# Sorting the first mixture's rows by expert, through DRAM, in a decoder layer of one core

## The chip, the core and the metric

The kernel runs on one core of a Trainium2 chip. A core has TensorE (PE, matmuls and transposes into PSUM), VectorE (DVE), ScalarE (ACT), GpSimd (POOL) and SyncE (SP, which here only issues DMAs), each with a queue of its own that runs in order; they wait for each other by semaphores. The time is the device time of one launch in microseconds; the runs given are separate launches.

## The reference, cut to what matters

`x` holds 16 sequences of 128 tokens of 128 features, 2048 tokens in all. Each of the three parts works on a layer norm of `x` and is added to `x`: a state-space layer with a mixture of 4 experts (below), cross-attention, and a second mixture of 8 experts (two for each token, with capacities), of 512 hidden units each.

```python
ssm_out = jnp.swapaxes(ys, 0, 1)              # the scan's output, 128 steps, 16 states
flat = ssm_out.reshape(-1, d)                 # 2048 x 128
routing = jax.nn.softmax(flat @ Wr + br, axis=1)
top1_w = jnp.max(routing, axis=1)
top1_i = jnp.argmax(routing, axis=1)
hid = jax.nn.silu(jnp.einsum('nd,edf->enf', flat, up_w) + up_b[:, None, :])
all_out = jnp.einsum('enf,efd->end', hid, down_w) + down_b[:, None, :]
sel = jnp.take_along_axis(jnp.swapaxes(all_out, 0, 1), top1_i[:, None, None], axis=1)[:, 0, :]
moe_out = (sel * top1_w[:, None]).reshape(Bb, Ll, d)
out = ssm_out + moe_out                       # then a layer norm
```

All four experts are computed for every token there, and one is chosen. Everything is float32.

## The kernel before, in words

The tokens are 16 tiles of 128, in `G` = 4 groups of `GT` = 4 tiles (512 tokens). The scan has 16 states for each group, 64 units in all. One slot k of a hand-written order stands for one unit: VectorE does `scan(k)`, `drive(k + 1)` (input times the broadcast row B) and `read_out(k - 1)` (state times the broadcast row C); TensorE makes the broadcasts (`send_B`, `send_C`, line 1389), two slots ahead for B; GpSimd adds each read-out to `yD` (`add_state`). `read_out(k)` waits until the sum three units back is made (`HC_RING` = 3). Each engine then does in `around(k)` what the tables `pre_at`, `mix_at`, `kv_at` and `att_at` put at this slot: preparation of the next group, the first mixture of the group just scanned, keys and values, attention and routing of the one before. Slots run on to 64 + 22 + 17 without units. Nothing but these tables and the queues sets the order.

The first mixture of group g begins at slot 16(g + 1) + 1, step 0. Its logits are one matmul a tile, `route_first` finds each token's best expert, and `gate_first` makes a gate of 4 columns that is zero but for the chosen expert. TensorE computes all experts for all tokens: 16 up matmuls of 512 columns, one a slot (`up`, line 1398), each followed by a SiLU on ScalarE (`silu`, line 1202), and 16 down tiles of four matmuls (`down`, line 1407), one a slot. `acc` starts as `yD` turned to rows plus gate times bias (lines 1488 and 1490), and VectorE adds gate times output for each expert at steps 9, 13, 17 and 21 (`add_expert`, line 593). The layer norm of `acc`, attention step 0, follows at step 21 in the same slot. All weights are loaded once at the start, into `w1` and `w2`.

For the last two groups the attention's steps are packed by `LATE_STEPS`. Its pieces are `inverse_root` on GpSimd, `normalize` on ScalarE, transposes, scores, exponentials. GpSimd also issues the second mixture's dispatches, indirect DMAs from `xrow` to `slots_in` (line 1060).

## Time and profile before

| | |
|---|---|
| median of 3 runs | 476.17 us (474.03 to 477.69) |
| the profiled execution's own time | 482.02 us |
| its span, first to last instruction | 480.2 us |
| TensorE's mean granted clock | 0.885 of 2.4 GHz |
| busy: PE, DVE, ACT, POOL | 344.7, 292.0, 263.0, 230.6 us |
| DMA traffic | 23.94 MB |

Busy time is summed over the records of an engine without overlap. TensorE's clock is granted at one of two levels, 1.2 or 2.4 GHz (0.5 and 1.0 in the tables); a number between is a stretch with both. A record of a float32 matmul is one of two that the instruction leaves. Times in the rows are microseconds from the span's start.

### The profile page before, as it was taken

How to read it: one execution, taken by the hardware profiler on the slowest of the kernel's cores; microseconds unless marked ns; L12 is line 12 of the kernel's file. 1: busy time of each engine (PE TensorE's matmuls, PEld its weight loads, DVE VectorE, ACT ScalarE, POOL GpSimd, SP SyncE). 2: the span in 40 equal slices, each digit the busy share in tenths (PEclk: the TensorE clock that was granted, in tenths of full speed). 3: DMA queues.
4: the chain of work that ended last, by engine and by line, in shares of the span. 5: the costliest groups of instructions: out<-in, count | busy, mean ns of one | idle time of the engine just before them, and what ended most of it. 6: DMA issues, size and time to landing. Idle time of an engine off the chain costs nothing. (4 is left out here: it accounts for less than half of the span.)

```text
span 480.2 us, 5947 instructions
## 1 busy us (share of the span) xinstructions
PE 344.7 (72%) x1749; PEld 233.6 (49%) x1749; DVE 292.0 (61%) x840; ACT 263.0 (55%) x465; POOL 230.6 (48%) x275
## 2 busy tenths in 40 slices
PE   1427557769896899978999688661537789999460
PEld 0203333346464565645667455561327757767360
DVE  3478988956999799999974245357136012222055
ACT  3554645668887797868537675413224474554021
POOL 4425755543545665464541422716844435455434
PEclk9999965879999899999899988975558899999966
DMA  6999400000000000000000000200120221210243
GB/s 123 290 233 333 124 1 1 0 0 1 1 1 0 2 1 1 1 2 0 1 1 2 0 0 9 81 1 23 50 61 28 77 67 49 76 53 14 78 120 88
DMA packets 29472, 23.94 MB, mean 50 GB/s; under 512 B 5448, under 2 KB 23943, under 8 KB 29440
## 3 DMA queue, kind: packets, MB, share of 16 engines
q1 hardware_dynamic: 27048, 19.50, 14.8%
q0 software_dynamic: 2304, 4.04, 2.5%
q8 instruction: 14, 0.23, 0.2%
q14 instruction: 18, 0.15, 0.1%
q10 hardware_dynamic: 88, 0.03, 0.0%
...
## 5 line engine op out<-in xcount | busy, mean ns | idle before, releaser
L1072 POOL TENSOR_TENSOR yD<-yD,hc 128x512 f32<-128x512 f32 x64 | 84.4, 1318 | 103.5 <-DVE hc L537 97.9
L1398 PE MATMUL bank<-yD,w 128*128 128x512 f32 x128 | 71.9, 645 | 17.1 <-ACT hid L1202 16.2
L502 DVE TENSOR_TENSOR_SCAN h<-a,bank 128x512 f32<-128x512 f32 x64 | 77.8, 1216 | 1.4 <-DVE bank L489 0.5
L1407 PE MATMUL bank<-w,hid 128*128 128x128 f32 x512 | 74.6, 293 | 0.0
L1407 PEld LDWEIGHTS bank<-w,hid 128*128 128x128 f32 x512 | 68.6, 205 | 9.4 <-issue 6.1
L1389 PE MATMUL bank<-rows,selid 99*128 99x512 bf16 x128 | 47.5, 457 | 25.5 <-DVE hc L537 23.4
L1135 POOL DMA_INDIRECT y_rows<-yslot,dest x40 | 39.1, 977 | 37.6 <-DVE yslot L865 22.1
L1202 ACT ACTIVATE hid<-bank,cols 128x512 f32<-128x512 f32 x64 | 43.4, 683 | 18.0 <-PE bank L1398 11.9
L489 DVE TENSOR_TENSOR bank<-bank,u 128x512 f32<-128x512 f32 x64 | 43.8, 684 | 14.5 <-PE bank L1389 14.2
L1060 POOL DMA_INDIRECT slots_in<-xrow,posu x32 | 32.3, 1010 | 32.7 <-DVE locs L684 14.7
L1389 PEld LDWEIGHTS bank<-rows,selid 99*128 99x128 bf16 x128 | 12.8, 106 | 67.4 <-DVE hc L537 47.0
L537 DVE TENSOR_TENSOR hc<-h,bank 128x512 f32<-128x512 f32 x64 | 43.3, 677 | 0.9 <-PE bank L1389 0.9
L1181 ACT ACTIVATE a<-delta,A_sb 128x508 f32<-128x508 f32 x64 | 40.5, 707 | 0.1
L865 DVE TENSOR_TENSOR yslot<-bank,w 128x128 f32<-128x128 f32 x32 | 9.2, 292 | 47.8 <-PE bank L1643 46.6
L593 DVE SCALAR_TENSOR_TENSOR acc<-bank,gate,acc 128x128 f32<-128x128 f32 x64 | 18.0, 344 | 29.5 <-PE bank L1407 29.4
L1338 ACT ACTIVATE hid<-bank,cols 128x512 f32<-128x512 f32 x32 | 22.0, 687 | 24.4 <-PE bank L1643 17.0
L1187 ACT ACTIVATE xrow<-x_tok,nmr,rstd 128x128 f32<-128x128 f32 x48 | 19.7, 482 | 23.2 <-POOL nmr L1037 23.2
L1372 PE MATMUL bank<-ident,xrow 128*128 128x128 f32 x48 | 9.5, 331 | 31.7 <-ACT xrow L1187 31.6
L1398 PEld LDWEIGHTS bank<-yD,w 128*128 128x128 f32 x128 | 20.8, 204 | 20.7 <-ACT hid L1202 18.1
L1643 PE MATMUL bank<-fc,hid 128*128 128x128 f32 x256 | 30.1, 275 | 0.7 <-DVE yslot L865 0.7
L1643 PEld LDWEIGHTS bank<-fc,hid 128*128 128x128 f32 x256 | 29.4, 192 | 1.8 <-issue 1.8
L1631 PE MATMUL bank<-w,fc1T 128*128 128x512 f32 x64 | 29.2, 596 | 1.5 <-ACT w L1320 1.5
...
## 6 DMA issues: line engine op xcount, KB each, us to landing
...
y_rows<-yslot SPq DMA_DIRECT2D x8, 256.0 KB, 5.2
x_tok<-in_x_dram SPq DMA_DIRECT2D x4, 256.0 KB, 3.9
...
yD<-y_rows SPq DMA_DIRECT2D x4, 256.0 KB, 4.4
xT<-y_rows SPq DMA_DIRECT2D x4, 256.0 KB, 5.7
out_dram<-acc SPq DMA_DIRECT2D x4, 256.0 KB, 2.3
```

Source lines behind the costliest of these rows:

```text
L489: do(v.tensor_tensor(drive_of(k), drive_of(k), grp(u, g), ALU.mult))
L502: ins = v.tensor_tensor_scan(state_of(k), decay_of(k).rearrange("p j n -> p (j n)"), drive_of(k), 0.0, ALU.mult, ALU.add)
L537: do(v.tensor_tensor(read_of(k), state_of(k), bank[C_BANK][:, 0:width(k // NS)], ALU.mult))
L1060: pool.indirect_dma_start(slots_in[:], bass.IndirectOffsetOnAxis(ap=posu[:, r, i:i + 1], axis=0), xrow[:, i, :], None, bounds_check=SLOTS - 1,
L1072: pool.tensor_tensor(grp(yD, g), grp(yD, g), read_of(k), ALU.add).then_inc(summed, 1)
L1135: pool.indirect_dma_start(y_rows[:], bass.IndirectOffsetOnAxis(ap=to, axis=0), yslot[:, half, j * P:(j + 1) * P], None, bounds_check=2 * T ...
L1181: act.activation(decay_of(k)[:, :, 1:P], tiles3(grp(delta, g))[:, :, 1:P], ACT.Exp, scale=A_sb[:, s:s + 1]).then_inc(a_done, 1)
L1202: act.activation(hid[:, m % 2, f, 0:width(g)], bank[UP_BANKS[f % 2]][:, 0:width(g)], ACT.Silu, bias=cols[:, C_UPB + i:C_UPB + i + 1]).then ...
L1389: pe.matmul(bank[b][:, 0:width(g)], selid[:, row:row + 1].to_broadcast([3 * NROW, P]), rows[:, p % 2, at_col:at_col + width(g)], start=Tru ...
L1398: pe.matmul(bank[UP_BANKS[f % 2]][:, 0:width(g)], w1[:, e, f * P:(f + 1) * P], grp(yD, g), start=True, stop=True).then_inc(up_ps, 1)
L1407: ins = pe.matmul(bank[DOWN_BANK][:, j * P:(j + 1) * P], hid[:, m % 2, f, j * P:(j + 1) * P], w2[:, e, f, :], start=(f == 0), stop=(f == F ...
L1643: ins = pe.matmul(bank[4 + t % 2][:, 0:P], hid2[:, e % 2, f, j * P:(j + 1) * P], fc2[:, e, f, :], start=(f == 0), stop=(f == FT - 1))
```

## The change

A group's tokens are sorted by expert into 7 tiles of 128 rows (`MT` = 4 + 4 - 1, enough for any split), and each tile meets only its owner's weights. VectorE makes from a one-hot and two counting matmuls each token's place (`sposu`) and each tile's owner; GpSimd scatters the rows, four indirect DMAs to `srt_in` in DRAM; SyncE reads them back as `xs_tok`, TensorE turns them and ScalarE copies them to `xsT`; each tile takes 4 up matmuls of 128 columns, 4 SiLUs, a bias matmul and 4 down matmuls; the results go by `ys` to `srt_out`, from where four gathers bring the tokens' rows to `back`, and one `add_expert` adds them. `w1` and `w2` are rings of four tiles; SyncE reads a tile's owner into a register and fetches its weights (512 KB) by it, 14.7 MB in all instead of 2 MB. Ups stand at steps 10 to 16, downs at 11 to 17, evictions at 15 and 18, gathers at 19, the add at 23, and the attention starts 25 slots after a group's end instead of 22.

```diff
+MT = GT + E1 - 1
+W_RING = 4
...
+            def sort_places(g):
                 sl = gsl(g)
-                inverse_sum(g, 0)
-                link(one_hot(gate[:, sl, :], sl, 0, 0))
-                do(v.tensor_tensor(gate[:, sl, :], gate[:, sl, :],
-                                   rz[:, 0, sl].unsqueeze(2).to_broadcast([P, SIZES[g], 8]), ALU.mult))
-                at["gate", g] = n[0]
-            def add_expert(g, e):
-                v.wait_ge(dn_ps, downs(g, e + 1))
-                v.wait_ge(init_done, g + 1)
-                v.wait_ge(dve_done, at["acc", g, e - 1] if e else at["gate", g])
+                square = [P, E1, E1]
+                v.wait_ge(cnt_ps, g + 1)
+                cum = bank[MIX_BANK][:, 0:GT * E1].rearrange("p (i e) -> p i e", e=E1)
+                tot = bank[MIX_BANK][:, GT * E1:2 * GT * E1].rearrange("p (i e) -> p i e", e=E1)
+                link(v.tensor_reduce(count1[:], tot.rearrange("p i e -> p e i"), AX.X, ALU.add))
+                link(v.tensor_tensor(cmp1[:], count1[:].unsqueeze(2).to_broadcast(square),
+                                     rows128[:].unsqueeze(1).to_broadcast(square), ALU.is_gt))
+                link(v.tensor_reduce(tiles1[:], cmp1[:], AX.X, ALU.add))
+                link(v.tensor_tensor(cmp1[:], below[:], tiles1[:].unsqueeze(1).to_broadcast(square), ALU.mult))
+                link(v.tensor_reduce(first1[:], cmp1[:], AX.X, ALU.add))
+                link(v.tensor_scalar(off1[:, 0, :], first1[:], float(P), -1.0, ALU.mult, ALU.add))
+                for j in range(GT - 1):
+                    link(v.tensor_tensor(off1[:, j + 1, :], off1[:, j, :], tot[:, j, :], ALU.add))
+                link(v.tensor_tensor(loc1[:], off1[:], cum, ALU.add))
+                at["cnt", g] = n[0]
+                link(v.tensor_tensor(loc1[:], loc1[:], oh1[:], ALU.mult))
+                link(v.tensor_reduce(spos[:], loc1[:], AX.X, ALU.add))
+                link(v.tensor_copy(sposu[:, sl], spos[:]))
+                at["spos", g] = n[0]
+            def sort_owners(g):
+                wide = [P, MT, E1]
+                link(v.tensor_tensor(past1[:], first1[:], tiles1[:], ALU.add))
+                link(v.tensor_tensor(whose[:], iota8[:, 0:MT].unsqueeze(2).to_broadcast(wide),
+                                     past1[:].unsqueeze(1).to_broadcast(wide), ALU.is_ge))
+                link(v.tensor_reduce(owner[:], whose[:], AX.X, ALU.add))
+                link(v.tensor_scalar_min(owner[:], owner[:], float(E1 - 1)))
+                link(v.tensor_copy(owner_no[:, g, :], owner[0:1, :]))
+                at["owner", g] = n[0]
+                do(v.tensor_scalar(owner_col[:, g % 2, :], owner[0:8, :], slot_no[0:8, 0:1], None, ALU.is_equal))
+                link(v.tensor_tensor(whose[:], owner[:].unsqueeze(2).to_broadcast(wide),
+                                     iota8[:, 0:E1].unsqueeze(1).to_broadcast(wide), ALU.is_equal))
+                link(v.tensor_tensor(bias_of[:], whose[:].unsqueeze(2).to_broadcast([P, MT, FT, E1]),
+                                     cols[:, C_UPB:C_UPB + E1 * FT].rearrange("p (e f) -> p f e", f=FT)
+                                     .unsqueeze(1).to_broadcast([P, MT, FT, E1]), ALU.mult))
+                link(v.tensor_reduce(up_bias[:, g % 2, :, :], bias_of[:], AX.X, ALU.add))
+                at["up_bias", g] = n[0]
...
+            def add_expert(g):
+                v.wait_ge(gathered, 16 * GT * (g + 1))
                 for j, i in enumerate(tiles_of(g)):
-                    do(v.scalar_tensor_tensor(acc[:, i, :], bank[DOWN_BANK][:, j * P:(j + 1) * P],
-                                              gate[:, i, e:e + 1], acc[:, i, :], ALU.mult, ALU.add))
-                at["acc", g, e] = n[0]
+                    do(v.scalar_tensor_tensor(acc[:, i, :], back[:, j, :], rz[:, 0, i:i + 1], acc[:, i, :],
+                                              ALU.mult, ALU.add))
+                at["acc", g] = n[0]
...
+            def weights(g, j, e):
+                t = g * MT + j
+                r = t % W_RING
+                if t >= W_RING:
+                    sp.wait_ge(dn_ps, t - W_RING + 1)
+                load(w1[:, r, :], up_w[bass.ds(e, 1), :, :].rearrange("e d f -> d (e f)"), ld_wt[r])
+                load(w2[:, r, :, :], down_w[bass.ds(e, 1), :, :].rearrange("e (t p) d -> p (e t) d", p=P), ld_wt[r])
+            for g in range(G):
+                sp.wait_ge(dve_done, at["owner", g])
+                for j in range(MT):
+                    if j == W_RING:
+                        sp.wait_ge(sorted_in, 16 * GT * (g + 1))
+                        if g:
+                            sp.wait_ge(xs_ps, g)
+                        load(xs_tok, srt_in[g][:].rearrange("(j p) d -> p j d", p=P), ld_rows)
+                    weights(g, j, sp.value_load(owner_no[0:1, g, j:j + 1], min_val=0, max_val=E1 - 1))
+                for half, (lo, hi) in enumerate(((0, GT), (GT, MT))):
+                    sp.wait_ge(evicted, 2 * g + half + 1)
+                    load(srt_out[g][lo * P:hi * P, :].rearrange("(j p) d -> p j d", p=P), ys[:, lo:hi, :], st_rows)
...
+            def sort_rows(g):
+                if g == 0:
+                    pool.wait_ge(cleared, 16 * 2 * G)
+                pool.wait_ge(yrow_done, g + 1)
+                pool.wait_ge(dve_done, at["spos", g])
+                for i in tiles_of(g):
+                    pool.indirect_dma_start(srt_in[g][:], bass.IndirectOffsetOnAxis(ap=sposu[:, i:i + 1], axis=0),
+                                            acc[:, i, :], None, bounds_check=SORTED - 1,
+                                            oob_is_err=False).then_inc(sorted_in, 16)
+            def fetch_rows(g):
+                pool.wait_ge(st_rows, 16 * 2 * (g + 1))
+                if g:
+                    pool.wait_ge(dve_done, at["acc", g - 1])
+                for j, i in enumerate(tiles_of(g)):
+                    pool.indirect_dma_start(back[:, j, :], None, srt_out[g][:],
+                                            bass.IndirectOffsetOnAxis(ap=sposu[:, i:i + 1], axis=0),
+                                            bounds_check=SORTED - 1, oob_is_err=False).then_inc(gathered, 16)
...
+            def silu(g, j):
+                t = g * MT + j
+                act.wait_ge(up_ps, t + 1)
+                if j == 0:
+                    act.wait_ge(dve_done, at["up_bias", g])
+                if t >= 2:
+                    act.wait_ge(dn_ps, t - 1)
+                for f in range(FT):
+                    ins = act.activation(hid[:, t % 2, f, 0:P], bank[UP_BANKS[t % 2]][:, f * P:(f + 1) * P], ACT.Silu,
+                                         bias=up_bias[:, g % 2, j, f:f + 1])
+                ins.then_inc(hid_done, 1)
+            def take_out(g, half):
+                lo, hi = (0, GT) if half == 0 else (GT, MT)
+                act.wait_ge(dn_ps, g * MT + hi)
+                if g:
+                    act.wait_ge(st_rows, 16 * 2 * g)
+                act.activation(ys[:, lo:hi, :], tiles3(bank[DOWN_BANK][:, 0:(hi - lo) * P]), ACT.Copy
+                               ).then_inc(evicted, 1)
...
+            def up(g, j):
+                t = g * MT + j
+                b = bank[UP_BANKS[t % 2]]
+                pe.wait_ge(xsT_done, 2 * (g + 1))
+                pe.wait_ge(ld_wt[t % W_RING], 32 * (t // W_RING + 1))
+                if t >= 2:
+                    pe.wait_ge(hid_done, t - 1)
                 for f in range(FT):
-                    ins = pe.matmul(bank[DOWN_BANK][:, j * P:(j + 1) * P], hid[:, m % 2, f, j * P:(j + 1) * P],
-                                    w2[:, e, f, :], start=(f == 0), stop=(f == FT - 1))
+                    ins = pe.matmul(b[:, f * P:(f + 1) * P], w1[:, t % W_RING, f * P:(f + 1) * P],
+                                    xsT[:, j * P:(j + 1) * P], start=True, stop=True)
+                ins.then_inc(up_ps, 1)
+            def down(g, j):
+                t = g * MT + j
+                o = bank[DOWN_BANK][:, j % GT * P:(j % GT + 1) * P]
+                pe.wait_ge(hid_done, t + 1)
+                if j == 0 and g:
+                    pe.wait_ge(evicted, 2 * g)
+                if j == GT:
+                    pe.wait_ge(evicted, 2 * g + 1)
+                pe.matmul(o, owner_col[0:E1, g % 2, j:j + 1].to_broadcast([E1, P]), bias1[0:E1, :],
+                          start=True, stop=False)
+                for f in range(FT):
+                    ins = pe.matmul(o, hid[:, t % 2, f, 0:P], w2[:, t % W_RING, f, :],
+                                    start=False, stop=(f == FT - 1))
                 ins.then_inc(dn_ps, 1)
...
```

The order on VectorE at the first group's slot 21 (step 4). Before, with `bcm` the preparation of another group:

```order
L436 TENSOR_TENSOR bcm<-bank,bbc_b 128x4x32 [waits rows_ps,ld_w,bc_ps]
L440 TENSOR_REDUCE bcm<-bcm 128x4 [waits dve_done]
L577 TENSOR_REDUCE zs<-ex 128x4 [waits dve_done,ex_done0]
L578 RECIPROCAL rz<-zs 128x4 [waits dve_done]
L561 TENSOR_TENSOR gate<-ixf,iota 128x32 [waits dve_done]
L584 TENSOR_TENSOR gate<-gate,rz 128x32 [waits dve_done]
L502 SCALAR_TENSOR_TENSOR h<-a,bank 128x512 [waits dve_done,a_done]
```

And now:

```order
L624 TENSOR_REDUCE count<-bank 128x4 [waits cnt_ps,dve_done]
L625 TENSOR_TENSOR cmp<-count,rows 128x16 [waits dve_done]
L627 TENSOR_REDUCE tiles<-cmp 128x4 [waits dve_done]
L628 TENSOR_TENSOR cmp<-below,tiles 128x16 [waits dve_done]
L629 TENSOR_REDUCE first<-cmp 128x4 [waits dve_done]
L630 TENSOR_SCALAR off<-first 128x4 [waits dve_done]
L632 TENSOR_TENSOR off<-off,bank 128x4 [waits dve_done] x3
L633 TENSOR_TENSOR loc<-off,bank 128x16 [waits dve_done]
L635 TENSOR_TENSOR loc<-loc,oh 128x16 [waits dve_done]
L636 TENSOR_REDUCE spos<-loc 128x4 [waits dve_done]
L637 CAST sposu<-spos 128x4 [waits dve_done]
L644 TENSOR_TENSOR past<-first,tiles 128x4 [waits dve_done]
```

The gate's two instructions gave way to this chain; eight more for the owners and biases follow, and only then the next scan.

TensorE in the last group's mixture, beside the scores of group 2 (L1536, now L1684). Before:

```order
L1407 MATMUL bank<-w,hid 128x128 [waits dve_done,hid_done]
L1407 MATMUL bank<-w,hid 128x128 x3
L1398 MATMUL bank<-yD,w 128x512 [waits hid_done]
L1536 MATMUL bank<-delta,yD 128x128 [waits k_done,dve_done]
L1536 MATMUL bank<-delta,yD 128x128 x3
```

And now:

```order
L1556 MATMUL bank<-bias,owner_col 128x128 [waits hid_done]
L1559 MATMUL bank<-w,hid 128x128 x4
L1544 MATMUL bank<-xsT,w 128x128 [waits hid_done,ld_wt0,xsT_done]
L1544 MATMUL bank<-xsT,w 128x128 x3
L1684 MATMUL bank<-delta,yD 128x128 [waits k_done,dve_done]
L1684 MATMUL bank<-delta,yD 128x128 x3
```

The down tile of four (L1407) got a bias matmul (L1556) ahead of it, and the up matmul of 512 columns (L1398) became four of 128 (L1544) that wait for the tile's weights and for `xsT`.

GpSimd behind the scan's last add, slots 65 to 71, with `inverse_root` as L1029 to L1037, now L1131 to L1139. Before:

```order
L1072 TENSOR_TENSOR yD<-yD,hc 128x512 [waits dve_done,summed] x5
L1029 TENSOR_SCALAR vpe<-mv 128x4 [waits dve_done]
L1030 TENSOR_SCALAR nmr<-mv 128x4
L1033 TENSOR_TENSOR rstd<-vpe,nhalf 128x4 [waits root_done]
L1037 TENSOR_TENSOR nmr<-nmr,rstd 128x4 [waits root_done]
L1112 COPY acc<-xrow 128x512 [waits normed3]
L1020 TENSOR_TENSOR x_tok<-x_tok,affine 128x512 [waits biased4]
```

And now:

```order
L1195 TENSOR_TENSOR yD<-yD,hc 128x512 [waits dve_done,summed] x2
L1183 DMA back<-srt_out,sposu 128x128 [waits dve_done,st_rows]
L1183 DMA back<-srt_out,sposu 128x128 x3
L1173 DMA srt_in<-acc,sposu 896x128 [waits dve_done,yrow_done]
L1173 DMA srt_in<-acc,sposu 896x128 x3
L1131 TENSOR_SCALAR vpe<-mv 128x4 [waits dve_done]
L1132 TENSOR_SCALAR nmr<-mv 128x4
L1135 TENSOR_TENSOR rstd<-vpe,nhalf 128x4 [waits root_done]
L1139 TENSOR_TENSOR nmr<-nmr,rstd 128x4 [waits root_done]
L1239 COPY acc<-xrow 128x512 [waits normed3]
```

The gathers of group 2, which wait for its store (`st_rows`), and the scatters of group 3 now stand ahead of group 1's `inverse_root`.

## Rows read from the trace of the kernel before

**Rows 1.** The page, its head: busy time of each engine

```profile
span 480.2 us, 5947 instructions
...
PE 344.7 (72%) x1749; PEld 233.6 (49%) x1749; DVE 292.0 (61%) x840; ACT 263.0 (55%) x465; POOL 230.6 (48%) x275
```

**Rows 2.** Busy time by stage, with clock, DMA share, GB/s

```profile
31.00:80.00 49.00, 28.36 (x86) 13.68 (x87) 46.11 (x63) 25.25 (x41) 27.62 (x25) 0.82 0.47 141
80.00:250.00 170.00, 146.94 (x736) 92.31 (x735) 149.49 (x324) 123.40 (x189) 87.15 (x89) 0.94 0.00 1
250.00:322.00 72.00, 58.60 (x324) 43.39 (x323) 29.78 (x163) 38.60 (x72) 22.25 (x31) 0.91 0.04 16
```

**Rows 3.** Who VectorE waited for, 80 to 250 us: total, times, longest

```profile
DVE bank L489 <- PE bank L1389: 13.1, 13, 4.9
DVE acc L593 <- PE bank L1407: 3.9, 6, 1.3
```

**Rows 4.** Groups by form, whole span: busy us, mean ns, idle before

```profile
L1407 PE MATMUL bank<-w,hid 128*128 128x128 f32 x512 | 74.6, 293 | 0.0
L1398 PE MATMUL bank<-yD,w 128*128 128x512 f32 x128 | 71.9, 645 | 17.1 <-ACT hid L1202 16.2 <-POOL yD L1072 0.5 <-issue 0.4
...
L1202 ACT ACTIVATE hid<-bank,cols 128x512 f32<-128x512 f32 x64 | 43.4, 683 | 18.0 <-PE bank L1398 11.9 <-PE bank L1407 5.3
```

**Rows 5.** The chain of waits from 353 us: start, us, what

```profile
353.03 2.28 DMA slots_in<-xrow,posu
...
355.33 3.83 DMA xe_early<-slots_in
...
361.28 1.84 PE bank L1602 x8
...
363.14 1.15 ACT hid L1313 x4
...
364.33 1.16 PE bank L1591 x8
365.49 0.91 PE bank L1602 x8
```

**Rows 6.** VectorE in order of time: start, us, what, idle before

```profile
213.31 1.18 DVE L561 TENSOR_TENSOR gate<-ixf,iota 128x32 f32<-128x32 f32 x1
...
251.27 0.69 DVE L537 TENSOR_TENSOR hc<-h,bank 128x512 f32<-128x512 f32 x1 [0.92 <-PE bank L1389]
...
320.47 1.13 DVE L593 SCALAR_TENSOR_TENSOR acc<-bank,gate,acc 128x128 f32<-128x128 f32 x4 [3.48 <-PE bank L1407]
...
322.95 0.78 DVE L653 TENSOR_TENSOR off<-off,bank 128x16 f32<-128x16 f32 x4
```

**Rows 7.** One line, all its instructions: ns min, median, max; first and last start

```profile
L502 DVE TENSOR_TENSOR_SCAN h<-a,bank x64: 1207/1214/1222, 31.2 to 248.0; 128x512 f32<-128x512 f32 x64
...
L1060 POOL DMA_INDIRECT slots_in<-xrow,posu x32: 969/974/1637, 297.0 to 373.8; - x32
```

**Rows 8.** GpSimd in order of time

```profile
213.17 1.27 POOL L1072 TENSOR_TENSOR yD<-yD,hc 128x512 f32<-128x512 f32 x1
...
326.76 1.64 POOL L1060 DMA_INDIRECT slots_in<-xrow,posu  x1 [1.82 <-DVE locs L684]
328.70 0.97 POOL L1060 DMA_INDIRECT slots_in<-xrow,posu  x1 [0.30 <-issue]
```

**Rows 9.** ScalarE in order of time

```profile
253.49 1.28 ACT L1229 ACT_TABLE_LOAD   x1
...
256.31 1.28 ACT L1202 ACT_TABLE_LOAD   x1
...
281.17 1.65 ACT L1187 ACTIVATE xrow<-x_tok,nmr,rstd 128x128 f32<-128x128 f32 x4 [3.27 <-POOL nmr L1037]
```

**Rows 10.** The page's DMA issues: KB each, us to landing

```profile
out_dram<-acc SPq DMA_DIRECT2D x4, 256.0 KB, 2.3
```

**Rows 11.** Busy time and clock in the tail

```profile
284.00:288.00 4.00, 4.00 (x15) 3.04 (x15) 0.49 (x2) 3.76 (x7) 0.15 (x1) 0.55 0.00 0
```

203 lines of the change are left out of this document (117 added, 86 removed).

## The prediction

> **What bounds the kernel now.** Read the page's first lines and then the table by stage [rows 1, 2]. TensorE is busy 72% of 480.2 us, which invites the thought that halving the mixture's matmuls must pay. The stages say otherwise. From 80 to 250 us, where the scan runs beside a group's mixture, VectorE is busy 149.5 of 170 us and TensorE 146.9: two engines are near their limit, and VectorE's list of waits holds what TensorE costs it, 13.1 us for the broadcasts and 3.9 us for the down matmuls [rows 3]. So in this stage less TensorE work can give 17.0 us at most, and more VectorE work takes back microsecond for microsecond. From 250 to 322 us TensorE is busy 58.6 of 72 us and VectorE 29.8: there the last group's mixture is bound by TensorE. After 322 us the kernel is not touched. The end of the last `add_expert` is the landmark: 320.47 + 1.13 = 321.6 us, which is 69.6 us after the last `read_out` ended at 251.27 + 0.69 = 251.96 [rows 6]. The page's chain of waits starts behind that landmark, so I count the time to it and take the 158 us behind it as they are.
>
> **What the change takes from TensorE.** One up matmul of 512 columns is two records of 645 ns in the mean, one down tile of four matmuls eight records of 293 ns; the starts are closer, since 71.9 and 74.6 us are busy for all 64 and all 64 [rows 4]. Per group that is 18.0 + 18.7 = 36.6 us of records. Instead come 7 tiles. The early feed-forward has the same shapes: four ups in 0.91 us, four SiLUs of 128 columns in 1.15, four downs in 1.16, all at full clock, and 1.84 for the ups at the lower clock [rows 5]. With a fifth matmul for the bias a tile is 0.91 + 1.16 x 5/4 = 2.4 us, a group 16.5, and the 11 transposes and two counts add about 1.3. TensorE is thus relieved of about 19 us a group. ScalarE's work is about even: 16 SiLUs of 683 ns [rows 4] against 28 in 7 x 1.15 = 8.1 us, and three or four evictions more.
>
> **The scan stage, 80 to 250 us.** (a) Waits that go. The longest broadcast wait, 4.9 us, stood where the first group's ups and ScalarE's table loads met; the ups now start ten slots later. It goes, and so do the 3.9 us of `add_expert`. Of the other 8.2 us I keep 7/16, since only 7 of 16 slots hold up and down matmuls: 3.6 us. Gain 17.0 - 3.6 = 13.4 us. (b) VectorE's own work. `choose_expert`, `sort_places` and `sort_owners` are 24 instructions for each group, nearly all chained, on 4 to 112 elements. Four chained ones took 0.78 us, 0.20 each [rows 6]; two wider ones I put at 0.27: 4.9 us, and 0.5 for operands in SBUF while GpSimd adds. (The 32-element one-hot took 1.18 us at 213.31, exactly until GpSimd's add of 213.17 to 214.44 ended [rows 6, 8].) Three groups pay 16.2 us. Out go eight of the ten `add_expert` in this stretch at 1.05 each (they overlap the next scan a little), 8.4 us, the gate's two instructions, 2.4 us over three groups with such waits in them, and one `row_max` that moves behind the scan, 0.6: net +4.8 us. (c) New waits. The chain from `sposu` to `xsT` is four scatters at 1.28, 2.3 to landing, a load that landed in 3.8 at a similar size [rows 5, 8], all in TensorE's queue ahead of the next broadcasts: about 12 us, against four slots of 2.3 (undisturbed) to 3.4 us (the mean of 63 steps from 31.2 to 248.0 [rows 7]). The ends are 0 and, if each group waits two slots, 15 us; I take 1.5 us a group, 4.5, near the low end because broadcasts are sent two slots ahead. Sum: -13.4 + 4.8 + 4.5 = **-4.1 us**.
>
> **The last group, walked by queue from t = 0, the last `read_out`.** Group 2's last down ends at 5, ScalarE evicts it at 7.7 behind the attention's exponentials (1.28 for the table; the next load starts 1.5 us behind it, after four [rows 9]), the store lands at 7.7 + 0.5 + 2.3 = 10.5 [rows 10]. GpSimd has waited for it: four gathers to 15.6, and only then, in its order, the four scatters of group 3 to 20.7. These land at 23.0, the load at 27.2, transposes and two copies end at 29.2. But the copies stand in ScalarE's queue behind a normalisation of group 2 (1.65 [rows 9]) that itself waits for GpSimd's root behind those scatters, so 31. Then seven tiles: TensorE needs 7 x 2.4 = 16.8, the attention of group 2 between them four blocks of 0.9, and ScalarE's queue puts in a normalisation, two table loads and the exponentials ahead of SiLUs, some 5 us: last down at 57. The second `take_out` stands in ScalarE's queue behind `normalize(3, 2)`, which waits for GpSimd's root (1.8), which waits for the eight dispatches of the second mixture (8 x 1.28 = 10.2, from about 46.5): out at 60.7. (The root's 1.8 is an estimate: a few small operations of GpSimd in a chain, between one add of 1.27 [rows 8] and two.) Store 2.8, gathers 5.1, landing 2.3, `add_expert` 1.1: 72.0. Before, 69.6: +2.4 us. This was at full clock. A window of the tail shows a clock of 0.55 with TensorE busy throughout [rows 11], and the walk has two waits of TensorE of more than 3 us. At the lower clock a tile takes some 2 us more, for about two tiles: +4. Sum: **+6.4 us** (from 0 to 15, if all seven tiles run at the lower clock).
>
> **The rest** counts at nothing: the 2 MB of weights no longer loaded at the start and the 1.8 MB that clear `srt_in` both lie under the first scans, whose first start at 31.2 us [rows 7] waits for no weights; cover gone would cost nothing either, as VectorE is busy 46.1 of the 49 us from 31 to 80 [rows 2]. The weights of each tile, 0.5 MB, are fetched four tiles ahead, over 7 us, against 3.8 us to landing for the same size [rows 5].
>
> Together -4.1 + 6.4 = +2.3 us on the profiled execution's 482.0: 484.3. The median of the runs stands at 476.17/482.02 = 0.988 of it: **478.4 us**. One per cent (4.8 us) is about what a measurement of this kernel can tell from no change.
>
> **Rivals.** *Faster.* TensorE was what held both stages, and the new waits find cover: (c) is 0 and nothing of the 8.2 us stays, 17.0 - 4.8 = 12.2 us gained; in the tail the clock holds, and `take_out` is not held behind the dispatches, 3 us less than walked, so -0.6. Time: (482.0 - 12.8) x 0.988 = 463.5 us. For it: TensorE at 58.6 of 72 us in the tail. Against: the walk's end hangs on GpSimd's and ScalarE's order, not on matmuls.
> *Much slower: GpSimd's queue.* GpSimd adds every unit's read-out to `yD`, and `read_out` waits for the add three units back. Four indirect DMAs in its queue hold it for 4 x 1.28 = 5.1 us, and with one add 6.4, less than three slots of 2.3 (63 instructions of VectorE in 49 us, three a slot [rows 2]): no wait. But one such instruction took 1.64 us where VectorE was busy with chained work, against 0.97 [rows 7, 8]. If all take 1.64 + 0.30, a batch holds GpSimd for 7.8 + 1.3 = 9.1 us, 2.1 more than three slots; five batches lie in the scan: +10.7. It decides from 1.4 us an instruction on. Time: (484.3 + 10.7) x 0.988 = 489 us, and 497 with the tail's upper end. For it: VectorE is busy nearly without a gap in the scan. Against: of the 32 such instructions the median is 0.974, the first of a batch alone was long. The Trainium skill's page "SBUF — State Buffer", section "SBUF: two separate sides", speaks against this change at this place: a DMA issued from GpSimd's queue cannot have its descriptors written while VectorE runs an instruction in a two-port mode, and the page advises the SP or ScalarE queue instead. By it the scan's broadcasts and scans are harmless and only copies or casts inside SBUF would hold it; the row of 1.64 shows that something does.
> *The work does not shrink:* matmuls of 128 columns cost what those of 512 did. The row of four ups in 0.91 us speaks against it. It would keep the 13.4 us in place: 492 us.
>
> **Chances.** Forecast, the terms nearly cancel, with its own range of 471 to 485: 0.45. Faster: 0.20. GpSimd's queue: 0.25. The work does not shrink: 0.03; something not on this list, mostly slower: 0.07. Of the forecast's 0.45, 0.33 lie within 1%, 0.10 above, 0.02 below. So faster 0.22, same 0.38, slower 0.40. The range runs from the faster rival to between the queue's two ends: 464 to 495.
>
> **What would show it.** Last scan: 4 us earlier than 248.0 [rows 7] if (a) to (c) are right, 12 earlier for the faster rival, later for the queue's; VectorE's waits would then name GpSimd's add. The distance from the last `read_out` to the end of `add_expert`: 76 us. In it GpSimd's gathers should wait for the store, the scatters stand right behind them, and the second `take_out` behind the normalisation. TensorE's busy time should fall by some 70 us or less, as the clock is lower. Wrong would make me: weights landing late (TensorE waiting on a load of `w`), indirect DMAs that take longer to land while weights stream, or a clock low for whole groups.

## The result: slower by a tenth, and the profile after

The changed kernel takes 523.6 us against 476.9 before. Three of its four runs lie from 522.3 to 524.0 us and one, a slow run that is left out of the ratio, at 537.8. The ratio is 1.098, with an interval of 1.091 to 1.105. Its profiled execution took 523.99 us, 42.0 more than the 482.02 of the one before, with a span of 522.1. The landmarks of [rows 6, 7] part these 42 us:

| us | before | after | forecast for after |
|---|---|---|---|
| last scan starts | 248.0 | 275.7 | 4.1 earlier than before |
| last `read_out` ends | 252.0 | 281.7 | |
| from there to the end of the last `add_expert` (the tail) | 69.6 | 86.9 | 76 |
| from there to the end of the span | 158.6 | 153.4 | 158.6 |

So 29.8 us came in the scan and 17.3 in the tail, and 5.2 went behind it, where nothing was changed. A part of these 5.2 us lies with the profiled execution of the kernel before, whose last stretch was long: in the fourteen experiments, those built on the kernel before among them, this last stretch took 151.0 to 156.3 us.

The page's head and the table by stage of the changed kernel are to be laid beside [rows 1, 2]:

```profile
span 522.1 us, 6051 instructions
...
PE 317.9 (61%) x1585; PEld 228.8 (44%) x1585; DVE 294.6 (56%) x882; ACT 240.3 (46%) x511; POOL 262.6 (50%) x307
...
31.00:80.00 49.00, 26.57 (x86) 12.76 (x85) 46.34 (x63) 24.58 (x41) 27.61 (x25) 0.87 0.48 149
80.00:250.00 170.00, 109.25 (x492) 74.43 (x492) 125.67 (x294) 88.68 (x172) 86.29 (x83) 0.68 0.25 70
250.00:322.00 72.00, 45.74 (x244) 35.46 (x245) 41.97 (x147) 30.35 (x78) 36.68 (x46) 0.69 0.31 89
```

From 31 to 80 us nothing moved. From 80 to 250 us TensorE is busy 109 us instead of 147, and VectorE, which should have had more time, only 125.7 instead of 149.5. The mean granted clock fell from 0.94 to 0.68. A mean over sparse records is rough; the broadcasts show the clock better, 0.60 us for the two records of one at full clock and about 1.04 at the lower. Of those that the timeline shows as a pair between scans 18 and 63, 5 of 45 took the long time before and 29 of 45 after.

VectorE's waits from 80 to 283 us, then TensorE's, are to be laid beside [rows 3]:

```profile
DVE bank L519 <- PE bank L1532: 35.4, 9, 8.8
DVE hc L567 <- PE bank L1532: 3.6, 1, 3.6
```

```profile
PE bank L1532 <- DVE hc L567: 40.0, 22, 7.0
PE bank L1556 <- ACT xe_tok L1340: 9.8, 2, 5.0
PE bank L1544 <- ACT xsT L1416: 6.2, 3, 4.1
PE bank L1556 <- ACT hid L1331: 4.4, 2, 2.2
```

The wait for broadcasts was to shrink from 13.1 us; it is 35.4, in 9 waits. TensorE in turn waits for ScalarE: 9.8 us for the eviction (`ys`, which the trace names `xe_tok`, whose memory it shares, as `xs_tok` shares that of `xe_early`), 6.2 us for the turned rows, 4.4 us for SiLUs. The starts of the scans tell where. The seven slots with tiles, scans 28 to 35 and 44 to 51, take 41.3 and 39.0 us; before, the same scans took 23.7 and 25.8. That is +17.6 and +13.3, together 30.8, more than the 27.7 us by which the last scan is late; scans 0 to 28, 35 to 44 and 51 to 63 changed by -6.3, +3.0 and -0.5.

The longest slot of the first stretch, around the first group's fifth tile, by ScalarE, TensorE and VectorE:

```profile
139.71 1.28 ACT L1308 ACT_TABLE_LOAD   x1
141.01 2.54 ACT L1308 ACTIVATE a<-delta,A_sb 128x508 f32<-128x508 f32 x4
143.57 1.28 ACT L1331 ACT_TABLE_LOAD   x1
144.87 1.14 ACT L1331 ACTIVATE hid<-bank,up_bias 128x128 f32<-128x128 f32 x4
145.88 0.61 ACT L1340 ACTIVATE xe_tok<-bank 128x512 f32<-128x512 f32 x1
...
140.29 1.06 PE L1544 MATMUL bank<-xsT,w 128*128 128x128 f32 x8
141.18 0.60 PE L1532 MATMUL bank<-rows,selid 99*128 99x512 bf16 x2
146.64 0.76 PE L1556 MATMUL bank<-bias,owner_col 4*128 4x128 f32 x2 [4.86 <-ACT xe_tok L1340]
147.33 2.08 PE L1559 MATMUL bank<-w,hid 128*128 128x128 f32 x8
149.20 1.91 PE L1544 MATMUL bank<-xsT,w 128*128 128x128 f32 x8
150.91 1.06 PE L1532 MATMUL bank<-rows,selid 99*128 99x512 bf16 x2
...
143.02 1.21 DVE L532 TENSOR_TENSOR_SCAN h<-a,bank 128x512 f32<-128x512 f32 x1
152.00 0.70 DVE L519 TENSOR_TENSOR bank<-bank,u 128x512 f32<-128x512 f32 x1 [7.77 <-PE bank L1532]
```

ScalarE first loads a table and makes four decays, loads the SiLU's table back, does the tile's SiLUs, and only then `take_out` evicts tiles 0 to 3 (145.88). TensorE's fifth down (its bias matmul, L1556) goes to the same bank and waits 4.86 us for that. When it goes on it is at the lower clock: 2.08 us for a down that otherwise takes 1.16. The next ups and the broadcasts stand behind it in TensorE's queue, and VectorE, idle since its scan at 143.02, waits 7.77 us. Of these, some 2.5 us are the clock's by an estimate from the rows: bias, down, ups and broadcast take 0.76 + 2.08 + 1.91 + 1.06 us here, and 0.48 + 1.16 + 1.06 + 0.60 where the clock is full. The second group's wait at the same place is 4.98 us for TensorE and 8.79 for VectorE.

The tail, by GpSimd, ScalarE, TensorE and VectorE, to be laid beside [rows 6, 8, 9]:

```profile
299.18 1.16 POOL L1183 DMA_INDIRECT back<-srt_out,sposu  x1 [16.02 <-DMA srt_out<-xe_tok]
...
304.56 1.02 POOL L1173 DMA_INDIRECT srt_in<-acc,sposu  x1 [0.30 <-issue]
...
309.59 0.23 POOL L1131 TENSOR_SCALAR vpe<-mv 128x4 f32<-128x4 f32 x1
...
360.93 1.18 POOL L1183 DMA_INDIRECT back<-srt_out,sposu  x1 [1.34 <-DMA srt_out<-xe_tok]
...
311.57 1.65 ACT L1314 ACTIVATE xrow<-x_tok,nmr,rstd 128x128 f32<-128x128 f32 x4 [13.83 <-POOL nmr L1139]
...
356.05 1.65 ACT L1314 ACTIVATE xrow<-x_tok,nmr,rstd 128x128 f32<-128x128 f32 x4 [4.45 <-POOL nmr L1139]
357.60 0.47 ACT L1340 ACTIVATE xe_tok<-bank 128x384 f32<-128x384 f32 x1
...
313.36 1.09 PE L1515 MATMUL bank<-ident,xrow 128*128 128x128 f32 x4 [13.50 <-ACT xrow L1314]
...
319.73 3.69 PE L1544 MATMUL bank<-xsT,w 128*128 128x128 f32 x16 [1.13 <-ACT xsT L1416]
...
367.55 1.14 DVE L663 SCALAR_TENSOR_TENSOR acc<-back,rz,acc 128x128 f32<-128x128 f32 x4 [3.60 <-DMA back<-srt_out,sposu]
```

The order of the walk is there: group 2's gathers wait for the store (16.02 us idle), four scatters stand behind them, group 1's root and normalisation (311.57) behind those, the first ups of the last group at 319.73, and the second `take_out` (357.60) right behind a normalisation that waited for GpSimd. Counted from the last `read_out`, at 281.75, the first gather is at 17.4 (the walk had 10.5), the last down ends at 72.7 (57), the eviction at 76.3 (60.7), the add at 86.9 (72.0).

### The profile page after: what moved, and what is told of

It reads as the page before. It is cut to its first block, busy times and chain, and to the rows that moved or that the text cites. A ratio compares the mean times of both kernels' runs of the same rounds, so it can differ in the third digit from the quotient of the medians.

```text
span 522.1 us, 6051 instructions
## 1 busy us (share of the span) xinstructions
PE 317.9 (61%) x1585; PEld 228.8 (44%) x1585; DVE 294.6 (56%) x882; ACT 240.3 (46%) x511; POOL 262.6 (50%) x307
## 3 DMA queue, kind: packets, MB, share of 16 engines
q1 hardware_dynamic: 55880, 37.59, 25.7%
## 4 chain that ended last, share of the span: by engine, by line
PE 33%; DVE 20%; issue 15%; ACT 14%; POOL 10%; DMA 6%; DVEq 1%; SPq 0%; POOLq 0%; ACTq 0%
PE bank L1791 5%; PE bank L1779 5%; PE bank L1559 4%; PE bank L1544 4%; ACT a L1308 3%; DVE h L532 3%; DVE bank L519 2%; POOL rstd L1135 2%; PE bank L1532 2%; DVE hc L567 2%; ACT hid L1331 2%; ACT L1331 2%; PE bank L1556 1%; ACT xrow L1314 1%; POOL srt_in L1173 1%
## 5 line engine op out<-in xcount | busy, mean ns | idle before, releaser
L1532 PE MATMUL bank<-rows,selid 99*128 99x512 bf16 x128 | 57.9, 548 | 58.9 <-DVE hc L567 56.6
L519 DVE TENSOR_TENSOR bank<-bank,u 128x512 f32<-128x512 f32 x64 | 44.0, 687 | 36.4 <-PE bank L1532 36.1
L1532 PEld LDWEIGHTS bank<-rows,selid 99*128 99x128 bf16 x128 | 13.1, 113 | 81.7 <-DVE hc L567 77.6
L1544 PE MATMUL bank<-xsT,w 128*128 128x128 f32 x224 | 40.5, 342 | 7.4 <-ACT xsT L1416 7.4
L1544 PEld LDWEIGHTS bank<-xsT,w 128*128 128x128 f32 x224 | 37.9, 255 | 9.4 <-ACT xsT L1416 9.0
L1515 PE MATMUL bank<-ident,xrow 128*128 128x128 f32 x48 | 11.2, 378 | 48.6 <-ACT xrow L1314 48.6
L1331 ACT ACTIVATE hid<-bank,up_bias 128x128 f32<-128x128 f32 x112 | 31.9, 373 | 19.0 <-PE bank L1544 18.9
L1308 ACT ACTIVATE a<-delta,A_sb 128x508 f32<-128x508 f32 x64 | 40.5, 707 | 0.1
L1559 PE MATMUL bank<-w,hid 128*128 128x128 f32 x224 | 37.7, 320 | 0.0
L1559 PEld LDWEIGHTS bank<-w,hid 128*128 128x128 f32 x224 | 31.8, 219 | 3.8 <-issue 0.9
L1481 ACT ACTIVATE hid<-bank,cols 128x512 f32<-128x512 f32 x32 | 22.0, 687 | 24.4 <-PE bank L1779 24.4
L1515 PEld LDWEIGHTS bank<-ident,xrow 128*128 128x128 f32 x48 | 7.8, 194 | 52.5 <-issue 26.9
L1791 PEld LDWEIGHTS bank<-fc,hid 128*128 128x128 f32 x256 | 29.4, 192 | 1.0 <-issue 1.0
```

Of the source, the lines that this page charges most:

```text
L519: do(v.tensor_tensor(drive_of(k), drive_of(k), grp(u, g), ALU.mult))
L1308: act.activation(decay_of(k)[:, :, 1:P], tiles3(grp(delta, g))[:, :, 1:P], ACT.Exp, scale=A_sb[:, s:s + 1]).then_inc(a_done, 1)
L1331: ins = act.activation(hid[:, t % 2, f, 0:P], bank[UP_BANKS[t % 2]][:, f * P:(f + 1) * P], ACT.Silu, bias=up_bias[:, g % 2, j, f:f + 1])
L1532: pe.matmul(bank[b][:, 0:width(g)], selid[:, row:row + 1].to_broadcast([3 * NROW, P]), rows[:, p % 2, at_col:at_col + width(g)], start=Tru ...
L1544: ins = pe.matmul(b[:, f * P:(f + 1) * P], w1[:, t % W_RING, f * P:(f + 1) * P], xsT[:, j * P:(j + 1) * P], start=True, stop=True)
L1559: ins = pe.matmul(o, hid[:, t % 2, f, 0:P], w2[:, t % W_RING, f, :], start=False, stop=(f == FT - 1))
```

## The experiments

Each ran beside the kernel before, whose median was 474.4 to 476.8 us. Landmarks are those of the profiled executions; 28-35 and 44-51 are the times between these scans, the slots with tiles; the rest is the time from the last add to the end of the span. All times are us.

| run | median us | last scan | 28-35 | 44-51 | tail | rest |
|---|---|---|---|---|---|---|
| before | 476.9 | 248.0 | 23.7 | 25.8 | 69.6 | 158.6 |
| after | 523.6 | 275.7 | 41.3 | 39.0 | 86.9 | 153.4 |
| e1 no tiles | 492.8 | 250.0 | 24.8 | 28.5 | 78.0 | 156.3 |
| e2 before, half the matmuls | 475.4 | 251.9 | 24.0 | 29.4 | 65.8 | 151.0 |
| e3 first eviction first | 515.9 | 268.4 | 32.5 | 36.1 | 83.9 | 153.9 |
| e4 filled | 547.7 | 285.0 | 42.9 | 38.5 | 97.4 | 153.8 |
| e5 e3 and SiLUs first | 502.6 | 256.9 | 28.1 | 27.4 | 83.4 | 153.9 |
| e6 e5 and downs later | 511.7 | 262.2 | 30.9 | 29.5 | 83.1 | 154.1 |
| e7 no trip | 512.1 | 276.2 | 40.3 | 39.4 | 78.8 | 151.5 |
| e8 e6 and scatters first | 516.8 | 267.3 | 35.8 | 30.8 | 85.4 | 155.5 |
| e9 before, lag 25 | 494.6 | 255.6 | 23.7 | 27.2 | 79.5 | 153.7 |
| e10 no tiles, no trip | 481.3 | 251.3 | 24.3 | 28.5 | 69.8 | 154.6 |
| e11 e5 and tail reordered | 500.3 | 254.4 | 27.6 | 27.4 | 82.0 | 153.7 |
| e12 e10, lag 22 | 475.6 | 249.2 | 22.8 | 25.5 | 64.7 | 151.7 |
| e13 e11, lag 23 | 501.1 | 262.9 | 24.1 | 29.1 | 74.4 | 152.8 |
| e14 e11, lag 22 | 518.1 | 270.0 | 24.1 | 26.9 | 81.3 | 155.5 |

### e1: the tiles' arithmetic out

```diff
-                    ins = pe.matmul(b[:, f * P:(f + 1) * P], w1[:, t % W_RING, f * P:(f + 1) * P],
-                                    xsT[:, j * P:(j + 1) * P], start=True, stop=True)
+                    if f == 0:
+                        ins = pe.matmul(b[:, 0:1], w1[:, t % W_RING, 0:P], xsT[:, j * P:j * P + 1],
+                                        start=True, stop=True)
...
+                act.activation(hid[:, t % 2, 0, 0:1], bank[UP_BANKS[t % 2]][:, 0:1], ACT.Copy).then_inc(hid_done, 1)
```

> The changed kernel with the tiles' arithmetic left out: an up is one matmul of one column, a SiLU a copy of one column, a down the bias matmul alone. Sorting, scatters, weights, stores and gathers stay, and so do the order and all semaphores. Theory A (the tiles' own chain up, SiLU, down, eviction in the queues holds the broadcasts): the 30.9 us that the two stretches of seven slots with tiles lost go, the last scan starts near 248 us or earlier (before 248.0, changed 275.7), and with a shorter tail the time is 460 to 485. Theory B (the sorting chain and the trip through DRAM are late): the stretches stay long, last scan above 265, time above 505.

The ratio to before is 1.036 (1.029 to 1.043). The last scan starts at 250.0, 2.0 us behind the kernel before, and both stretches are short again: theory A, for the scan. The time is above its 485, since the tail is still 78.0. The run takes the SiLUs out with the matmuls, and with them nearly all of ScalarE's table loads (from scan 28 to the last, 2 instead of 15), so by itself it doesn't tell TensorE's share from ScalarE's; e3 and e5 do. The table by stage, from 80 us to the last scan and in the tail:

```profile
80.00:250.01 170.01, 111.11 (x345) 62.16 (x345) 150.78 (x356) 68.31 (x141) 104.00 (x106) 0.52 0.27 80
256.27:334.27 78.00, 39.71 (x143) 30.05 (x142) 28.65 (x167) 19.20 (x60) 33.31 (x42) 0.50 0.32 95
```

TensorE is at the lower clock nearly throughout (42 of the 45 paired broadcasts between scans 18 and 63 are long), and yet the scan is only 2.0 us longer than before: where nothing waits for a tile, most broadcasts at the lower clock are in time.

### e2: half of TensorE's mixture out of the kernel before

```diff
+                n = width(g) if e < 2 else 16
+                pe.matmul(bank[UP_BANKS[f % 2]][:, 0:n], w1[:, e, f * P:(f + 1) * P], grp(yD, g)[:, 0:n],
...
+                n = FT if e < 2 else 1
+                for f in range(n):
```

> The kernel before with most of experts 2 and 3's matmuls left out: their ups are 16 columns wide and their down tiles one matmul of four. SiLUs, gates and adds stay. It takes some 14 us of TensorE's records from each group and moves nothing. The prediction's part (a) (waits for TensorE shrink with its work): last scan 6 to 12 us earlier than 248.0, tail some 5 us shorter, time 460 to 468. Theory C (less work lowers TensorE's clock, and what remains is slower): last scan within 3 us of 248.0, granted clock in the scan well below 0.94, time 472 to 480.

The ratio is 0.998 (0.995 to 1.002): no change. From 80 us to the last scan, and the mean durations of a broadcast's and a down's records:

```profile
80.00:251.87 171.87, 137.53 (x628) 89.58 (x626) 146.29 (x320) 121.23 (x186) 85.53 (x87) 0.80 0.00 1
...
L1409 PE MATMUL bank<-w,hid 128*128 128x128 f32 x320 | 57.7, 321 | 0.8 <-DVE acc L593 0.8
L1389 PE MATMUL bank<-rows,selid 99*128 99x512 bf16 x128 | 52.8, 503 | 36.3 <-DVE hc L537 34.2 <-DVE h L502 1.8
```

192 fewer records over the kernel, and TensorE is busy only 21 us less (323.6 for 344.7 [rows 1]). A record of a broadcast went from 457 to 503 ns in the mean and one of a down tile from 293 [rows 4] to 321. Of the paired broadcasts between scans 18 and 63, 16 of 45 are long instead of 5. VectorE's wait for them went up, not down, from 13.1 [rows 3] to 15.6 us. The time is theory C's, though the last scan is 3.9 us later where it had at most 3; only the tail gained, 3.8 us. The prediction's part (a) would have had the last scan 6 to 12 us earlier. That the clock is why the rest gained nothing is argued and not shown: no run held the clock up with the matmuls out.

### e3 and e5: the order in ScalarE's slot

```diff
+                if (g := mix_at(k, OUT_STEPS[0])) is not None:
+                    take_out(g, 0)
                 if (g := pre_at(k, 1)) is not None:
                     normalize(0, g, quads(g), xn, x_tok)
...
+                for j in range(MT):
+                    if (g := mix_at(k, UP_STEP + j)) is not None:
+                        silu(g, j)
                 if k % A_BATCH == 0:
                     for i in range(k + A_BATCH, k + 2 * A_BATCH):
```

e3 has the first two added lines (and `take_out(g, 1)` where both stood), e5 the second piece too, with `take_out(g, 1)` right behind it and the loops behind taken out.

> The changed kernel with the first eviction (take_out of tiles 0 to 3) at the head of its slot in ScalarE's queue, ahead of the decays and of the SiLUs of that slot. Theory A, in its eviction part: the two waits of TensorE of 4.9 and 5.0 us for it go, VectorE's 7.8 and 8.8 us for broadcasts shrink to 2 or 3, last scan 8 to 12 us earlier than 275.7, time 508 to 516. Theory B: within 3 us of 523.6.

> As the run with the first eviction at the head of its slot, and each tile's four SiLUs ahead of the decays in ScalarE's slot instead of behind them. Theory A, in its SiLU part: TensorE's waits for SiLUs of 2.2 us behind the decays go and the stretches of seven slots shrink from 32.5 and 36.1 us towards 25; last scan near 258, time 500 to 508. If only the eviction mattered: 513 to 518 as before this step.

Both times came as theory A had them, 515.9 and 502.6 us, and the ratio went from 1.098 to 1.087 and 1.059 (1.052 to 1.066). In the scan 7.3 us hung on the eviction, where 8 to 12 were expected, and 11.4 more on the SiLUs behind the decays. TensorE's waits for ScalarE up to the last scan confirm it: the 9.8 us for the eviction are gone in e3, and the waits of the downs for SiLUs, in e3's list first and then in e5's, go with the second step:

```profile
PE bank L1558 <- ACT hid L1331: 8.4, 5, 2.2
...
PE bank L1558 <- ACT hid L1331: 0.2, 1, 0.2
```

TensorE in e5, around the same tile, with the wait that is left for VectorE:

```profile
136.49 0.48 PE L1558 MATMUL bank<-bias,owner_col 4*128 4x128 f32 x2
136.90 1.16 PE L1561 MATMUL bank<-w,hid 128*128 128x128 f32 x8
137.90 1.06 PE L1546 MATMUL bank<-xsT,w 128*128 128x128 f32 x8
138.79 0.60 PE L1534 MATMUL bank<-rows,selid 99*128 99x512 bf16 x2
...
DVE bank L519 <- PE bank L1534: 13.8, 9, 3.6
```

No down waits for ScalarE in this stretch, and a down takes 1.16 us. VectorE's wait is 13.8 us, near the 13.1 of before. With 28.1 and 27.4 us for the stretches, 18.8 of the 25.7 us that the tiles cost the scan are given back by the order alone.

### e4: TensorE kept busy

```diff
+                for _ in range(FILL):
+                    pe.matmul(o, ident[:], ident[:], start=True, stop=True)
+                pe.wait_ge(hid_done, t + 1)
```

> The changed kernel with eight more matmuls of 128 columns (identity by identity, into the tile's own columns, overwritten by the bias matmul) ahead of each down tile's wait for its SiLUs: some 1.8 us of TensorE's time for each of 28 tiles at full clock, part of it in time in which it waited. Theory C (the low clock, 0.68 in the scan and 0.69 behind it, is what costs): clock in the scan above 0.85, time 505 to 518 in spite of the added work. Theory A: the fill stands in the same queue ahead of the broadcasts and is paid in part, time 525 to 545.

547.7 us, a little above theory A's range. The clock rose only from 0.757 to 0.787 over the span, and from 80 us to the last scan from 0.68 to 0.75, where theory C had it above 0.85. The stretches with tiles stayed about as long as they were (42.9 and 38.5); elsewhere the fill was paid. So this fill doesn't pay. As it didn't bring the clock up, it doesn't tell what a full clock would give, and theory C isn't refuted by it; that the clock isn't the main cost rests on e5, which gives back 18.8 us of the scan by the order alone, with 27 of 45 paired broadcasts still long.

### e6 and e8: the downs one slot later

```diff
-DOWN_STEP = UP_STEP + 1
+DOWN_STEP = UP_STEP + 2
...
-                if t >= 2:
-                    act.wait_ge(dn_ps, t - 1)
+                if t >= 4:
+                    act.wait_ge(dn_ps, t - 3)
```

e8 has also `fetch_rows(g - 1)` behind `sort_rows(g)` for the last group.

> As the reordered ScalarE queue, and each down tile one slot later, with four buffers for the SiLUs' results instead of two: three slots in TensorE's queue lie between an up and its down. Theory A: no down waits for a SiLU any more; the stretches of seven slots fall to the 25 and 28 us of the kernel without the tiles' arithmetic, last scan near 252, time 493 to 503. If the low clock alone makes the stretches long, they stay above 32 us and the time above 505.

> As the run with downs one slot later, and in GpSimd's queue the last group's four scatters ahead of group 2's four gathers instead of behind them. If GpSimd's order sets the last group's start: sorted rows are loaded some 5 us earlier, group 2's attention starts 5 us later, and the time falls by 1 to 5 us. If the attention of group 2, whose work stands in the same queues ahead of the tiles, sets it: no gain, or up to 4 us slower.

Both missed. e6 was slower than e5 by 9.1 us. With the downs, the first eviction moved from the slot of the decays to the one behind it, and so behind them again in ScalarE's queue:

```profile
139.22 2.54 ACT L1308 ACTIVATE a<-delta,A_sb 128x508 f32<-128x508 f32 x4
141.68 0.57 ACT L1340 ACTIVATE xe_tok<-bank 128x512 f32<-128x512 f32 x1
...
142.39 0.76 PE L1558 MATMUL bank<-bias,owner_col 4*128 4x128 f32 x2 [1.61 <-ACT xe_tok L1340]
143.09 2.08 PE L1561 MATMUL bank<-w,hid 128*128 128x128 f32 x8
144.96 1.06 PE L1534 MATMUL bank<-rows,selid 99*128 99x512 bf16 x2
```

TensorE waits 1.61 us and goes on at the lower clock. Scans 35 to 44, where no tile stands, take 44.1 us against e5's 40.5, so this wait is a part of the loss at most, and the rest is open. e8 differs from e6 only in GpSimd's queue behind the scan, and yet its last scan is 5.1 us later, and the medians of four runs are 5.1 apart with ranges that don't meet (509.0 to 514.4, and 516.4 to 516.8 with one run of 524.2). Its tail is 2.3 us longer, as the second guess had it, but why two builds with the same scan differ in it is open; a difference of 5 us between two such builds proves nothing here, which bears on the small differences of e11 to e13 below as well.

### e7 and e10: without the trip through DRAM

```diff
-                    pe.wait_ge(ld_rows, 16 * (g + 1))
+                    pe.wait_ge(yrow_done, g + 1)
...
-                                           xs_tok[:, j, :], ident[:])
+                                           acc[:, g * GT + j % GT, :], ident[:])
...
-                v.wait_ge(gathered, 16 * GT * (g + 1))
+                v.wait_ge(evicted, 2 * (g + 1))
```

> The changed kernel without the trips through DRAM: no scatters, no load of the sorted rows, no stores and gathers; the tiles are turned from the unsorted rows and the final add reads the evicted tiles. VectorE's sorting chain, the weights, ups, SiLUs and downs stay, so it computes with unsorted rows. Theory A: the scan is as long as in the changed kernel (last scan within 4 us of 275.7), since the tiles' chain sets it; the tail, 86.9 us, loses the gathers, stores and landings, 20 us or more, and falls to some 65; time 497 to 505. Theory B: last scan near 250 and time below 485.

> The changed kernel without the tiles' arithmetic and without the trips through DRAM; sorting on VectorE, the counts, the weights, the turn and all places in the order stay. Without tiles the tail was 78.0 us, without the trip 78.8, with both 86.9, before 69.6. If tiles and trip are paid one behind the other: tail near 70, last scan near 250, time 480 to 485. If both hide behind the same chain of attention, roots and sorting: tail 74 to 78, time 487 to 491.

e7's last scan is at 276.2, half a microsecond from the changed kernel's: the trip costs the scan nothing that can be seen. The last add of e7,

```profile
359.95 1.13 DVE L663 SCALAR_TENSOR_TENSOR acc<-xe_tok,rz,acc 128x128 f32<-128x128 f32 x4
```

ends 78.8 us after the last `read_out` at 282.25. So the trip costs the tail 8.1 us and not 20, and the time of 512.1 us is above what theory A had for it. e10, with tiles' arithmetic and trip both out, came as its first guess had it and settles the sum: the tail is 69.8 with neither, 78.8 with the tiles alone, 78.0 with the trip alone, 86.9 with both. The trip costs 8.2 us without the tiles and 8.1 with them, the tiles 9.0 without the trip and 8.9 with it: they stand one behind the other. And with neither, the kernel takes 481.3 us, 1.017 (1.005 to 1.028) of before: without a matmul of the mixture's tiles it isn't faster than the kernel that computes every expert.

### e9, e12, e13, e14: the lag of the attention

```diff
-        if k == NS * (g + 1) + 22 + at_step:
+        if k == NS * (g + 1) + 25 + at_step:
```

e12 to e14 go the other way, with `ATT_LAG` = 22 or 23 and `TURN_STEP` = 8, which puts the turn, the ups and the downs one slot earlier too; with the lag moves the add, to step 20 or 21.

> The kernel before with nothing changed but the start of a group's attention, 25 slots after the group's end instead of 22, as in the changed kernel: three slots more of attention work behind the last read_out. If that shift is what lengthened the tail by 17.3 us (69.6 to 86.9): tail 75 to 80, time 482 to 487. If the tail is long because sorting, its trip and the late start of the tiles stand in one chain: tail within 3 us of 69.6, time 474 to 480.

> As the run e10 (the changed kernel without tiles' arithmetic and without the trips, 481.3 us, tail 69.8 us, last scan 251.3), with the attention back at 22 slots behind the group's end, the add at step 20 and the turn, ups and downs one step earlier. If the three slots of lag cost what they cost the kernel before: tail near 60, last scan 245 to 249, time 465 to 470. If the lag is free here: time 479 to 484.

> As the run e11 (500.3 us, all arithmetic and trips), with the turn, the ups, the downs, the evictions and the gathers one step earlier and the attention at 23 slots instead of 25. If the lag costs 5 to 6 us a slot as in the kernel before: 488 to 492. If the gathers, three slots ahead of the add, are late in the scan and the tail is set by trip and tiles: 497 to 503.

> As e13, with the attention at 22 slots: the add stands two slots behind the gathers, some 4.6 us of undisturbed slots against 5.1 us of issuing and 2.3 to landing. Lag as dear as before: 483 to 488. Gathers late: VectorE waits some 3 us for them in each of three groups, 490 to 500.

The lag alone made the kernel before slower by 4.7%, 494.6 us, more than the 482 to 487 expected. The interval of 1.035 to 1.059 is wide because the kernel before spread from 469.9 to 478.3 us beside it. The last scan is 7.6 us later and the tail 9.9 longer, 79.5, which is in the range of the first guess. VectorE's waits in its scan:

```profile
DVE bank L489 <- PE bank L1389: 18.7, 15, 4.9
DVE acc L593 <- PE bank L1407: 7.5, 6, 2.4
```

Broadcasts cost 18.7 us instead of 13.1 and down tiles 7.5 instead of 3.9 [rows 3]; which pieces of one group's attention now meet which of the next group's mixture in TensorE's queue wasn't traced further. In the bare kernel three slots less of lag, with the turn one slot earlier, gave back 5.7 us (481.3 to 475.6; a ratio of 1.017 became 0.998 to before), which lies between the two guesses, with a tail of 64.7 for 69.8. In the full one it is a trade: e13's tail is 7.6 us shorter than e11's and its last scan 8.5 later, so the time is the same (second guess). e14 is 17.9 us slower than e11, above both its ranges. It isn't the gathers that make it so: VectorE's waits up to e14's last scan hold 2.7 us for them in all, against 20.2 for broadcasts, where e11 has 14.0:

```profile
DVE bank L519 <- PE bank L1536: 20.2, 14, 6.5
DVE acc L438 <- ACT acc L1316: 5.6, 2, 4.2
DVE acc L663 <- DMA back<-srt_out,sposu: 2.7, 2, 2.4
```

The turn one slot earlier has a share in both: at the first group TensorE waits 3.09 us in e13, and 3.1 in e14, for the load of the sorted rows, in the stretch from scan 0 to 28 that takes 88.1 us instead of e11's 81.7. How much of the whole is its own wasn't run apart.

### e11: the tail's queues

```diff
                     inverse_root(gsl(g), g, 3)
+                if (g := mix_at(k, 5)) == G - 1:
+                    sort_rows(g)
```

The two counting matmuls also stand ahead of `around_attention`.

> The reordered ScalarE queue of the run e5 (502.6 us), and in addition the two counting matmuls ahead of the attention's work in TensorE's slot, and the last group's scatters behind group 1's inverse root in GpSimd's. Group 1's last normalisation waited until GpSimd had issued four gathers and four scatters; it should start 3 to 5 us earlier, the scatters 2 us later. If that chain sets the tail: tail 79 to 81 instead of 83.4, time 498 to 501. If the last group's tiles set it: tail 84 to 86, time 503 to 506.

500.3 us, 2.3 less than e5, and a tail of 82.0 for 83.4. The time is in the first guess's range and the tail a little above it, but 2.3 us are less than two like builds differ by, so that this chain sets the tail isn't shown. e11 and e13 are the fastest versions with the sorting, and the runs don't tell them apart: 1.058 (1.047 to 1.070) and 1.052 (1.047 to 1.057) of before. None of the versions beats the kernel before.

## Why the prediction was wrong, point by point

**What bounds the kernel.** It read right that the scan stage is held by VectorE and that less TensorE work can give little there. It then took VectorE's waits for TensorE, 13.1 and 3.9 us, as a measure of TensorE's amount of work, **part (a), -13.4 us**. Of these, 8.8 us went as forecast: scans 0 to 28 gained 6.3 us, where the wait of 4.9 us had stood, and VectorE has no wait for the add left. What failed is the share of the other broadcast waits that was to go with the work, 4.6 us: they grew, and e2, with half the mixture's matmuls out at an unchanged order, got nothing, while the clock fell with the work. TensorE's busy time fell by 26.8 us and not by some 70.

**Part (b), VectorE's own work, +4.8 us**, was about right: 22 of the 24 instructions and two neighbours took 5.1 us in the first group (93.59 to 98.69), where the sum had 5.4 for the 24, and VectorE's busy time from 80 us to the last scan rose from 147.5 to 150.3. With tiles out (e1) the scan came 2.0 us later than before, against the 4.8 + 4.5 - 13.4 that the parts gave.

**Part (c), new waits, +4.5 us**, is the step that failed most. The forecast was +2.3 us and the profile has +42.0; of the 39.6 us between them, 33.9 lie in the scan (29.8 against -4.1), 10.9 in the tail (17.3 against 6.4) and -5.2 behind it. Part (c) looked for new waits in the trip: scatters, landing, load. There they were not: VectorE has one wait of 3.49 us at the first tile, and e7 without the trip is no earlier. It had no term for the tiles' own chain. Before, only every fourth down tile was the first to read new SiLUs, the last of them two slots back; now each does, one slot behind its SiLUs, and up, SiLU, down and the one bank's eviction follow each other, through ScalarE's queue, where the decays of every fourth slot with two tables take 5.1 us (1.28 + 2.54 + 1.28). Everything queued behind a waiting down pays, the broadcasts above all. The prediction counted ScalarE's work as even (16 SiLUs of 683 ns against 28 in 8.1 us) and didn't ask where in the slot they stand. The measured term is 25.7 us (275.7 to 250.0), of which the order gives back 18.8 (e5); what the other 6.9 are, amount of work, clock or what is left of the chain, is open.

**The tail, +6.4 us**, had its queue order right and its size wrong: 17.3. The walk had group 2's last down end at 5 us, and it ended at 12.2, so the gathers began 7 us later than walked and the last group's ups too, at 38 us instead of 31. From there to the last down it counted 26 us, and it took 34.7: TensorE waited 2.08, 1.94 and 2.97 us between the tiles, and four tiles' ups and two tiles' downs ran at the lower clock, which is some 5 us by the rows, near the 4 us that the prediction had for it. The walk also didn't see that the dense mixture's ups had filled TensorE's waits for the attention from the first slot on, while the tiles can start only at 38 us. e1, e7 and e10 give the sizes: trip some 8.2, tiles some 9, and 69.8 that are left with neither; what holds these 69.8 wasn't taken apart.

**The lag** got no term at all. "The attention starts 25 slots after" was read as where a step is put; e9 prices it, alone in the kernel before, at 4.7%. In the kernel without tiles and trip the same three slots, with the turn one slot earlier, are worth 5.7 us (e10, e12). How much of the changed kernel's 46.7 us is the lag's isn't shown: e13 and e14, with less of it, were no faster.

**The rivals.** GpSimd's queue didn't decide: its scatters took 0.99 us in the median and 1.21 at most, its gathers 1.00 and 1.18, under the 1.4 us from which it counts, and neither add nor read-out had a wait for them in the lists. Matmuls of 128 columns cost what was forecast (a down 1.16 us at full clock), and the weights were in time: TensorE's list names no wait for them. The rival that was missing is the one that held.
